# The first cross-attention's unit in another order on all engines

## The reference

```python
def _mha_cross(x, mem, in_w, in_b, out_w, out_b):
    ...
    q = _split_heads(x @ wq.T + bq, H)        # H = 16 heads of hd = 8
    k = _split_heads(mem @ wk.T + bk, H)      # mem: 1601 rows an item
    v = _split_heads(mem @ wv.T + bv, H)
    scores = jnp.einsum('bhqd,bhkd->bhqk', q, k) * (1.0 / math.sqrt(hd))
    attn = jax.nn.softmax(scores, axis=-1)
    out = _merge_heads(jnp.einsum('bhqk,bhkd->bhqd', attn, v))
    return out @ out_w.T + out_b
```

## Time and profile before

| what | us |
|---|---|
| median of 3 runs | 3433.33 |
| lowest and highest run | 3430.18, 3441.29 |
| profiled execution, time | 3437.91 |
| profiled execution, span from first to last instruction | 3436.0 |
| TensorE busy (share of the span) | 3282.3 (96%) |
| VectorE busy | 2386.2 (69%) |
| ScalarE busy | 1907.4 (56%) |
| GpSimd busy | 1612.3 (47%) |

### The profile page before, as it was taken

One profiled execution on the slowest core, in us unless ns is written; L12 is line 12 of the kernel. 1 busy time (PEld: TensorE's weight loads), 2 busy tenths in 40 slices (PEclk: granted clock), 3 DMA queues, 4 the chain that ended last, 5 costly groups with the idle time before them and its releaser, 6 DMA issues. The chain is left out here.

```text
span 3436.0 us, 67280 instructions
## 1 busy us (share of the span) xinstructions
PE 3282.3 (96%) x26181; PEld 1891.3 (55%) x26320; DVE 2386.2 (69%) x5439; ACT 1907.4 (56%) x2599; POOL 1612.3 (47%) x1271
## 2 busy tenths in 40 slices
PE   6899999999997898999999999999999998989999
PEld 4566666666655674555545555455544544655555
DVE  8778778778774536777777777777777775653333
ACT  6466666666664234666666666666666663432222
POOL 5433343333322104777777777777777764300000
PEclk8699999999999899999999999999999999989999
DMA  2133333333310002101111011110111101000000
GB/s 75 38 73 78 82 74 75 77 78 77 76 41 1 26 1 74 39 21 38 39 39 39 20 39 39 39 39 20 39 39 39 33 17 50 1 28 4 4 4 4
DMA packets 90541, 138.92 MB, mean 40 GB/s; under 512 B 14512, under 2 KB 67824, under 8 KB 89456
## 3 DMA queue, kind: packets, MB, share of 16 engines
q1 hardware_dynamic: 90224, 134.61, 14.5%
HBM read 94.15 MB, written 1.05 MB: 28 GB/s over the span
## 5 line engine op out<-in xcount | busy, mean ns | idle before, releaser
L2490 ACT ACTIVATE arena<-banks,arena 128x512 f32<-128x512 f32 x832 | 560.3, 687 | 476.6 <-PE banks L2279 476.6
L2304 PE MATMUL banks<-arena 128*128 128x512 f32 x1664 | 803.9, 603 | 0.8 <-ACT arena L2497 0.8
L2238 POOL TENSOR_TENSOR arena<-arena 128x1024 f32<-128x1024 f32 x256 | 603.8, 2359 | 165.7 <-ACT arena L2497 164.6
L1250 DVE TENSOR_REDUCE arena<-banks 128x1 f32<-128x512 f32 (+1 forms) x896 | 529.1, 627 | 162.5 <-PE banks L1084 157.9
L2392 DVE TENSOR_TENSOR banks<-arena,banks 128x512 f32<-128x512 f32 x640 | 444.3, 694 | 241.9 <-ACT arena L2490 221.1
L1390 ACT ACTIVATE arena<-banks 128x1024 f32<-128x1024 f32 (+1 forms) x448 | 423.7, 961 | 277.3 <-PE banks L1164 277.1
L2409 DVE TENSOR_TENSOR arena<-arena,banks 128x1024 f32<-128x1024 f32 (+1 forms) x448 | 507.2, 1133 | 1.6 <-PE banks L2294 1.2
L2497 ACT ACTIVATE arena<-arena 128x1024 f32<-128x1024 f32 (+1 forms) x448 | 443.0, 989 | 11.1 <-DVE arena L2409 10.9
L2304 PEld LDWEIGHTS banks<-arena 128*128 128x128 f32 x1664 | 289.9, 190 | 220.8 <-issue 200.3
L2279 PE MATMUL banks<-arena 128*128 128x512 bf16 x830 | 313.2, 377 | 2.5
L2278 PE MATMUL banks<-arena 128*128 128x512 bf16 x786 | 297.9, 379 | 4.1
(11 more groups left out here) (356 smaller groups left out, 5116.7 us busy)
## 6 DMA issues: line engine op xcount, KB each, us to landing
arena<-arena SPq DMA_DIRECT2D x768, 50.0 KB, 2.2
arena<-in_ctxT SPq DMA_DIRECT2D x32, 800.5 KB, 6.3
arena<-in_ctx SPq DMA_DIRECT2D x32, 768.0 KB
fold<-in_ctxT SPq DMA_DIRECT2D x16, 800.5 KB, 4.6
foldv<-in_ctxT SPq DMA_DIRECT2D x16, 800.5 KB, 4.7
arena<-in_m2w SPq DMA_DIRECT2D x3, 2048.0 KB, 8.0
arena<-in_xw SPq DMA_DIRECT2D x1, 2048.0 KB, 8.0
weights<-in_weights SPq DMA_DIRECT2D x1, 1920.0 KB, 11.5
```

What stands on the lines that cost most here:

```text
L1250: eng.tensor_reduce(o, s, AX, ALU.max).then_inc(a_max, 1)
L2238: eng.tensor_tensor(part, part, tiles, ALU.add).then_inc(sums, 1)
L2304: eng.matmul(c.ps[:, R_MIX + v % 2, :], ctxn[:, b, kt * D:(kt + 1) * D], st[:, v % 2, kt, :], start=kt == 0, stop=kt == KT - 1).then_inc(m ...
L2490: eng.activation(st[:, v % 2, kt, :], c.ps[:, n % SB, :], ACT.Identity, bias=hide[:, kt, v // 2:v // 2 + 1])\
```

## The change

In the first cross-attention alone, and only the order and the use of bank 7:

- The small chunk (65 rows) comes second and no longer last (`PARTS`), in the code ahead of the loop too.
- TensorE's unit is written out: the mixes 0 and 1, 2 and 3, 4 and 5 stand together, mix 6 alone. The chunks, maxima blocks and scores stand between.
- The final product, the queries and the small chunk stand one behind the other. They are put in different columns of bank 7 (small chunk from 0, queries from 128, final product from 384), and `share_bank7` lets them follow without a wait; the next use of the bank waits for all of them.
- VectorE does the final quotient and the queries behind the first maxima block, and before these it waits until ScalarE has read the small chunk. ScalarE reads the chunks 0 and 1 together behind its second exponential.
- The sum of shift and queries is formed on TensorE (two more products), VectorE only copies it.

```diff
-    chunks = [(0, 512), (512, 1024), (1024, 1536), (1536, S)]
+    PARTS = (0, 3, 1, 2)
+    chunks = [(512 * p, min(512 * p + 512, S)) for p in PARTS]
+    QAT, FAT = P, P + 4 * L
...
-        if held["until"] is not None:
-            eng.wait_ge(*held["until"])
-        held["until"] = until
+        for freed in held["until"]:
+            eng.wait_ge(*freed)
+        held["until"] = [until]
+
+    def share_bank7(eng, until):
+        held["until"].append(until)
...
         def queries(i, b):
-            take_bank7(eng, (q_made, i * 2 + b + 1))
-            pe_query(eng, i, b, 7)
+            share_bank7(eng, (q_made, i * 2 + b + 1))
+            pe_query(eng, i, b, 7, QAT)
...
-                mm = eng.matmul(o, lt[:, s2, :], unit, start=True, stop=True)
+                eng.matmul(o, lt[:, s2, :], unit, start=True, stop=False)
+                mm = eng.matmul(o, unit, q4a[:, v // 2, 2 * (v % 2) + s2, :], start=False, stop=True)
...
-                for st in range(STEPS):
-                    if st == STEPS - 1:
-                        mix(i, v, st)
-                    if st < 5:
+                old = i + v > 0
+
+                def other(n, bank7=take_bank7):
+                    if v % 2 == 0:
+                        if here(2):
+                            values(*((i, 1) if v == 0 else (i + 1, 0)), n, bank7)
+                    elif more:
+                        keys(i + 1, v // 2, n, bank7)
+
+                def highest(a):
+                    if a < STEPS:
                         if here(1):
-                            maxima(*later(i, v, 1), st + 2)
+                            maxima(*later(i, v, 1), a)
                     elif here(2):
-                        maxima(*later(i, v, 2), st - 5)
-                    if st < 4:
-                        n = st
-                        if v % 2 == 0:
-                            if here(2):
-                                values(*((i, 1) if v == 0 else (i + 1, 0)), n)
-                        elif more:
-                            keys(i + 1, v // 2, n)
-                    elif st == 4:
-                        if i + v > 0:
-                            final(*later(i, v, -1))
-                    elif st == 6 and v % 2 == 1 and more:
+                        maxima(*later(i, v, 2), a - STEPS)
+
+                other(0)
+                highest(2)
+                scores(i, v, 2)
+                mix(i, v, 0)
+                mix(i, v, 1)
+                if old:
+                    final(*later(i, v, -1))
+                    if v % 2 == 1 and more:
                         queries(i + 1, v // 2)
-                    if st < STEPS - 1:
-                        mix(i, v, st)
-                    if st < 5:
-                        scores(i, v, st + 2)
-                    if st == 5 and here(1):
-                        shifts(*later(i, v, 1))
+                other(1, share_bank7 if old else take_bank7)
+                highest(3)
+                scores(i, v, 3)
+                other(2)
+                highest(4)
+                scores(i, v, 4)
+                mix(i, v, 2)
+                mix(i, v, 3)
+                highest(5)
+                scores(i, v, 5)
+                other(3)
+                highest(6)
+                scores(i, v, 6)
+                mix(i, v, 4)
+                mix(i, v, 5)
+                highest(7)
+                if here(1):
+                    shifts(*later(i, v, 1))
+                mix(i, v, 6)
+                highest(8)
                 if here(1):
                     scores(*later(i, v, 1), 0)
                     scores(*later(i, v, 1), 1)
...
-            if v % 2 == 0:
-                eng.wait_ge(q_spread, i * 4 + v + 2)
-            eng.tensor_tensor(q4b[:, v % 2], c.ps[:, 7, 0:2 * P].rearrange("p (s q) -> p s q", q=P),
-                              q4a[:, v // 2, 2 * (v % 2):2 * (v % 2) + 2, :], ALU.add).then_inc(q4b_made, 1)
+            eng.tensor_copy(q4b[:, v % 2].rearrange("p s q -> p (s q)"), c.ps[:, 7, 0:2 * P]).then_inc(q4b_made, 1)
...
-                for st in range(STEPS):
-                    if st == 0 and old:
-                        mask_mix(*later(i, v, -1))
-                    if st < 5:
+
+                def highest(a):
+                    if a < STEPS:
                         if here(1):
-                            maxima(*later(i, v, 1), st + 2)
+                            maxima(*later(i, v, 1), a)
                     elif here(2):
-                        maxima(*later(i, v, 2), st - 5)
-                    if st == 4 and here(1):
-                        spread_max(*later(i, v, 1))
-                    if st == 4 and old:
-                        final(*later(i, v, -1))
-                    if st == 5 and here(1):
-                        add_shift(*later(i, v, 1))
-                    if st == 6 and v % 2 == 1 and more:
+                        maxima(*later(i, v, 2), a - STEPS)
+
+                if old:
+                    mask_mix(*later(i, v, -1))
+                highest(2)
+                if old:
+                    if v % 2 == 0:
+                        if here(2):
+                            eng.wait_ge(v_made, i * 8 + (6 if v == 0 else 10))
+                    elif more:
+                        eng.wait_ge(k_copied, (i + 1) * 8 + 4 * (v // 2) + 2)
+                    final(*later(i, v, -1))
+                    if v % 2 == 1 and more:
                         queries(i + 1, v // 2)
+                for a in range(3, STEPS):
+                    highest(a)
+                if here(1):
+                    spread_max(*later(i, v, 1))
+                highest(7)
+                if here(1):
+                    add_shift(*later(i, v, 1))
+                highest(8)
...
-                for st in range(STEPS):
-                    exps(i, v, st)
-                    if 1 <= st < 5:
-                        n = st - 1
-                        if v % 2 == 0:
-                            if here(2):
-                                values(*((i, 1) if v == 0 else (i + 1, 0)), n)
-                        elif more:
-                            keys(i + 1, v // 2, n)
+
+                def other(n):
+                    if v % 2 == 0:
+                        if here(2):
+                            values(*((i, 1) if v == 0 else (i + 1, 0)), n)
+                    elif more:
+                        keys(i + 1, v // 2, n)
+
+                exps(i, v, 0)
+                exps(i, v, 1)
+                other(0)
+                other(1)
+                exps(i, v, 2)
+                exps(i, v, 3)
+                other(2)
+                exps(i, v, 4)
+                exps(i, v, 5)
+                other(3)
+                exps(i, v, 6)
```

More of the change, by code:

```diff
@@ L1043, in pool @@
         pairs(eng, body)
-    held = {"until": None}
+    held = {"until": []}
     def take_bank7(eng, until):
-        if held["until"] is not None:
-            eng.wait_ge(*held["until"])
-        held["until"] = until
+        for freed in held["until"]:
[3 more added lines that the diff above has]
+        held["until"].append(until)
     def pe_key(eng, i, b, n, bank):
@@ L1060, in pe_value @@
     def pe_value(eng, i, b, n, bank):
-        for kt in range(4 * n, min(4 * n + 4, KT)):
+        for kt in range(4 * PARTS[n], min(4 * PARTS[n] + 4, KT)):
             w = P if kt < KT - 1 else KL
@@ L1065, in pe_value, with pe_query @@
         mm.then_inc(v_ps, 1)
-    def pe_query(eng, i, b, bank):
+    def pe_query(eng, i, b, bank, at=0):
         for s in range(4):
-            mm = eng.matmul(c.ps[:, bank, s * L:(s + 1) * L], c.W("c_wq", s * P, (s + 1) * P),
+            mm = eng.matmul(c.ps[:, bank, at + s * L:at + (s + 1) * L], c.W("c_wq", s * P, (s + 1) * P),
                             c.xT[:, i, b * L:(b + 1) * L], start=True, stop=True)
@@ L1118, in pe, with keys, values @@
     def pe(eng):
-        def keys(i, b, n):
-            take_bank7(eng, (k_copied, i * 8 + 4 * b + n + 1))
+        def keys(i, b, n, bank7=take_bank7):
+            bank7(eng, (k_copied, i * 8 + 4 * b + n + 1))
             pe_key(eng, i, b, n, 7)
-        def values(i, b, n):
-            take_bank7(eng, (v_made, i * 8 + 4 * b + n + 1))
+        def values(i, b, n, bank7=take_bank7):
+            bank7(eng, (v_made, i * 8 + 4 * b + n + 1))
             pe_value(eng, i, b, n, 7)
         def queries(i, b):
-            take_bank7(eng, (q_made, i * 2 + b + 1))
-            pe_query(eng, i, b, 7)
+            share_bank7(eng, (q_made, i * 2 + b + 1))
+            pe_query(eng, i, b, 7, QAT)
         def maxima(i, v, a):
@@ L1145, in final @@
             r = slice(v % 2 * L, v % 2 * L + L)
-            for at, a, b in ((0, "num_a", "num_b"), (L, "den_a", "den_b")):
+            for at, a, b in ((FAT, "num_a", "num_b"), (FAT + L, "den_a", "den_b")):
                 eng.matmul(c.ps[r, 7, at:at + L], c.C(a), s1, start=True, stop=False)
@@ L1231, in pe, with dve_query @@
         final(PAIRS - 1, UNITS - 1)
```

(17 more changed lines are left out.)

## The result

The changed kernel took 3543.28 us (median of 4 runs, 3541.15 to 3547.04) beside 3433.43 for the kernel before (4 runs, 3430.18 to 3441.29). The ratio is 1.0311, 95% interval 1.0295 to 1.0327. So it is 110 us slower where 31 were forecast: the sign is right, the size is a third. The profiled execution took 3541.15. The edited stage, from its first shift to its last, went from 857.8 to 962.0 us; the rest of the kernel stayed (2578.2 and 2577.3).

What follows compares the result with a forecast made beforehand. TensorE was taken to set the pace. Per pair of units, waits +1.53 and switches -0.66 gave +0.87, taken as 0.9: 32 x 0.9 = 29 us, plus 2 for the clock, so 3464 us against 3433.3; range 3415 to 3495.

Steps and rivals of the forecast that it cites:

- The added wait, +1.94 a pair: At shared bank 7, TensorE's next whole chunk waits for all three results to be read: 1.17 + 0.77 us a pair.
- The switches, -0.66: TensorE's own work a pair: joined mixes -0.84, queries' place -0.14, maxima block apart +0.10, shift's sum +0.22 us.
- The +0.22 for the shift's sum: On TensorE, four more products of 128 columns a pair in the shift were to add 0.22 us.
- The sum, +0.9 a pair and 3464 us: Waits +1.53 and switches -0.66 give +0.87 a pair, taken as 0.9; with the clock's +2, 3464 us.
- the waits at a unit's end: TensorE at the last maxima blocks and shift: 0.5 of waiting plus 0.13 late, 0.65 a unit, 1.30 a pair.
- ScalarE and GpSimd keep their room. The copies of the keys stand at the same places: ScalarE (17.4 of 27.2 us busy) and GpSimd (10.2) keep their room; key copies stay between the units; no cost added.
- The clock, +2 with room for 20: One more fall of TensorE's clock to half from longer waits, +2 us, with room for a dozen, 20 us.
- Rival 3: Slower than forecast: joined mixes wait for weights, +0.6 a pair, or a dozen more clock falls, 3484 to 3490; chance 0.14.
- Rival 1: Faster: ScalarE reads the small chunk early, the added wait costs nothing and switches count, -0.8 a pair, 3408; chance 0.16.
- Rival 2's sum: It cancels: switches cost half as much again, stalls 1.4 in place of 1.94, leaving +0.3 a pair, 3441; chance 0.10.

Runs made afterwards that it cites:

- experiment 1: The changed kernel, but GpSimd splits the fourth (whole) key chunk only after VectorE has made the maxima into the shift's operand: 3465.81 us, ratio 1.0073.
- experiment 2: The changed kernel with six products of unused result added on TensorE ahead of every second unit's late shift: 3508.31 us, ratio 1.0201.
- experiment 4: The kernel before, with only the sum of shift and queries moved to TensorE (two more products) and VectorE copying: 3437.77 us, ratio 0.9988.
- experiment 7: Experiment 6 with TensorE reordered: shift's sum on VectorE again, final product behind mixes 0 and 1, mixes 3 and 4 joined: 3410.36 us, ratio 0.9918.
- experiments 5 and 6: 5: changed kernel, old chunk order, bank 7 taken in turn, no VectorE wait for ScalarE, GpSimd held before third chunk, 3451.29 us; 6: without GpSimd's wait, 3461.29.
- experiment 3: The kernel before, with only the small chunk moved to second place (`PARTS`), its order otherwise kept: 3502.91 us, ratio 1.0184.

## Why the prediction was right in sign and wrong in size

By its own steps, with the whole kernel's ladder beside: 3439 (before), 3466 (experiment 1), 3508 (experiment 2), 3543 (after, from the session in which before was 3433).

- **The added wait, +1.94 a pair: right.** 0.68 and 1.07 are 1.75 in place of 1.94. The walk itself had come to 1.2 to 1.3 and 0.8, and 1.17 and 0.77 were taken without a reason given; either is near. VectorE's reciprocal stood 1.23 and 2.17 for ScalarE (forecast 1.2 and 2.1), in these rows of the first and second unit:

```profile
507.44 0.56 DVE L1338 RECIPROCAL arena<-banks 64x64 f32<-64x64 f32 x1 [1.23 <-ACT arena L1398]
...
521.84 0.55 DVE L1338 RECIPROCAL arena<-banks 64x64 f32<-64x64 f32 x1 [2.17 <-ACT arena L1388]
```

- **The switches, -0.66: the joins right** (1.01 for two mixes, in every join of the pair; twice 0.58 less 0.14 is 1.02). The +0.22 for the shift's sum was mis-sized: it is hidden behind a wait for VectorE, and alone it showed as -0.1 a pair (experiment 4).
- **The sum, +0.9 a pair and 3464 us: right for what it held.** Experiment 1 has the order, the shared bank and the wait, without the block, at 28.08 and 3466. It isn't luck: the waits at a unit's end, forecast at 0.65 each, are 0.64 and 0.57 in it (from a maxima block to the scores 0.87 and 0.80, where 0.23 is undisturbed).
- **"ScalarE and GpSimd keep their room. The copies of the keys stand at the same places": the step that failed.** It costed the move of the small chunk by GpSimd's busy share alone. The busy share did stay (10.23, after 10.30). But which instructions of VectorE GpSimd's split runs beside changed: the shift then waits 1.63 us, and that term, put at nothing, is 42 us. The price should have come from VectorE's instructions beside the split, and not from how busy the engines are.
- **The clock, +2 with room for 20: the second step that failed.** I saw the fall behind an idle time in the earlier trace rows and didn't ask whether the new idle time comes in every pair. 26 falls fewer are 35 us less (experiment 2). It isn't independent of the first: without the block there are 5 falls.
- **Rival 3** named a clock that falls a dozen times more, for +20; the mechanism was half right, and its other half (joined mixes waiting for their weights) didn't occur. **Rival 1** (faster, 3408) is what the order gives once the waits are gone: 26.13 and 3410 in experiment 7, beside the 26.2 to 26.4 worked out for it. But it needed another order, not a faster ScalarE, so this doesn't bear the rival out. (3408 was 26 us under 3433; the 3410 is 30 under 3440.)
- **Rival 2's sum** is off: 0.87 less 0.42 for the switches and 0.54 for the stalls is about -0.1 a pair, and not +0.3; nothing else hangs on it.

Open: experiments 5 and 6 differ from 7 in several moves at once, so which of those is worth what wasn't told apart. The shared bank's wait is read from the rows; no run takes out that alone. That idle time at one place brings most of the falls is shown; why 14 falls in experiment 3 and 29 after, is not.

## What to carry to other kernels

When a change moves work of GpSimd in time, list what VectorE runs beside it at the new place: here a small cast and a product with both inputs in SBUF, on the path to TensorE, took five times as long, and the engines' busy shares say nothing of it. Count a wait of TensorE that recurs in every turn of a loop twice, once as time and once as a possible fall of the clock, and test that with products put in the gap whose result is not used. Of the joins, the shared bank and the moved chunk only the joins shortened anything, by 0.15 us each. The kernel gained in one order of the three without the added wait (experiment 7, not 5 and 6): the one in which neither a late shift nor late copies held TensorE up.

## What the runs showed of the hardware that I had not expected

- A cast of four columns took 0.93 us in place of 0.17 and a product of 64 columns 1.07 in place of 0.23, both until GpSimd's instruction was over. Reductions from the products' memory (1.29) and a copy from it (0.41, experiment 1) were not stretched beside the same work.
- Idle time of 1.6 us at one place, in a loop in which TensorE counts 27.19 of 30.72 us as busy, went with a fall of the granted clock to 0.5 for 3.40 us behind it, once a turn; with products for 1.24 us in the gap 3 falls were left of 29, and the mean granted clock of the stage went from 0.94 to 0.99.
- A wait put on GpSimd to keep it off VectorE gave 77 us in one order (experiment 1), and in another it gave 10 (5 against 6): there it stood ahead of the third chunk and not the fourth, for 3.00 us and not 2.00, and TensorE waited 75.7 us in the stage for the late copies in place of 7.2.
